# VectorE takes the low halves 4 to 7 in one row with the second norm's statistics behind them, and GpSimd adds the last layer's residual one step later

## What is computed

```python
h = maximum(_layernorm(x), 0);  x = x + elu(softmax(masked leaky_relu(f1 + f2)) @ h)       # first block
h = maximum(_layernorm(x), 0);  y = h
for l in range(3):                                                                       # second block
    attn = softmax(where(mask, leaky(si + sj + b), -inf))
    z = layernorm(y + attn @ y) * g1 + beta1                                             # first norm
    ff = gelu(z @ W1[l] + b1) @ W2[l] + b2
    y = layernorm(z + ff) * g2 + beta2                                                   # second norm
return x + y                                                                             # the residual
```

## Time and profile before

| | us |
|---|---|
| median of three runs | 2756.68 |
| lowest and highest | 2756.49, 2758.12 |
| the profiled execution | 2756.02 |
| its span in the profile | 2754.2 |
| granted TensorE clock, mean | 0.987 |

### The profile page before, as it was taken

How to read it: one execution, slowest core, us unless ns; L and a number is a source line. 1 busy time by engine, 2 the same in 40 slices (tenths; PEclk the granted TensorE clock), 3 DMA queues, 4 the chain that set the end, 5 groups by cost and what they waited for, 6 DMA issues and landing times.

```text
span 2754.2 us, 53331 instructions
## 1 busy us (share of the span) xinstructions
PE 2652.4 (96%) x16771; PEld 2388.7 (87%) x16868; DVE 2139.7 (78%) x7999; ACT 2201.9 (80%) x4494; POOL 1677.8 (61%) x2181
## 2 busy tenths in 40 slices
PE   4699999999999999999999999999999999999997
PEld 3688988898889898988898989898888898998997
DVE  6998787877787877787877888877888767677674
ACT  4889888888888888888887888888888777777774
POOL 4466666557676556566666566555676554454555
PEclk7899999999999999999999999999999999999999
DMA  6222222222122212122322121212132211111121
GB/s 203 75 73 85 70 94 73 77 74 94 63 93 66 77 64 74 51 76 81 100 74 88 45 81 66 78 56 89 60 104 81 68 36 52 42 46 53 50 64 54
DMA packets 118590, 203.43 MB, mean 74 GB/s; under 512 B 12801, under 2 KB 85537, under 8 KB 118305
## 3 DMA queue, kind: packets, MB, share of 16 engines
q1 hardware_dynamic: 118304, 199.97, 22.5%
HBM read 116.05 MB, written 83.89 MB: 73 GB/s over the span
## 4 chain that ended last, share of the span: by engine, by line
PE 72%; DVE 12%; POOL 8%; issue 5%; ACT 2%; DMA 1%; SPq 0%; DVEq 0%; POOLq 0%; ACTq 0%
PE bank L605 33%; PE bank L588 27%; PE ps_u L564 7%; POOL xo L374 3%; DVE g_lo L988 3%; DVE st L962 2%; POOL rs L1295 2%; PE ps_u L646 2%; PE ps_s L559 2%; DVE ub L1081 2%; PE ps_s L551 1%; POOL hb L374 1%; DVE ub L957 1%; ACT g_hi L862 1%; ACT bank L864 1%
## 5 line engine op out<-in xcount | busy, mean ns | idle before, releaser
L605 PE MATMUL bank<-w_hi,g_hi 128*128 128x256 f32 x3072 | 890.9, 290 | 15.4 <-DVE g_lo L988 15.2
L605 PE MATMUL bank<-w_hi,g_lo 128*128 128x256 f32 x3072 | 865.8, 282 | 0.0
L605 PE MATMUL bank<-w_lo,g_hi 128*128 128x256 f32 x3072 | 864.4, 281 | 0.0
L862 ACT ACTIVATE g_hi<-bank,b_eff 128x512 fp32r<-128x512 f32 x768 | 529.7, 690 | 334.2 <-PE bank L588 327.9
L988 DVE TENSOR_TENSOR g_lo<-bank,g_hi 128x512 fp32r<-128x512 f32 x768 | 519.5, 687 | 201.5 <-ACT bank L864 186.2
L588 PE MATMUL bank<-zt_hi,w_hi 128*128 128x512 f32 x1536 | 632.6, 412 | 9.3 <-DVE g_lo L988 5.6
L588 PE MATMUL bank<-zt_hi,w_lo 128*128 128x512 f32 x1536 | 607.4, 395 | 0.0
L588 PE MATMUL bank<-zt_lo,w_hi 128*128 128x512 f32 x1536 | 606.3, 395 | 0.0
L605 PEld LDWEIGHTS bank<-w_hi,g_hi 128*128 128x128 f32 x3072 | 579.5, 189 | 24.1 <-DVE g_lo L988 22.9
L605 PEld LDWEIGHTS bank<-w_lo,g_hi 128*128 128x128 f32 x3072 | 579.8, 189 | 0.8
L605 PEld LDWEIGHTS bank<-w_hi,g_lo 128*128 128x128 f32 x3072 | 579.2, 189 | 0.0
(11 more groups left out here) (96 smaller groups left out, 4141.1 us busy)
## 6 DMA issues: line engine op xcount, KB each, us to landing
xb<-x_scratch SPq DMA_DIRECT2D x88, 512.0 KB, 4.0
x_scratch<-xo SPq DMA_DIRECT2D x64, 512.0 KB, 4.8
xin<-in_x SPq DMA_DIRECT2D x38, 512.0 KB, 4.7
r_scratch<-elu_r SPq DMA_DIRECT2D x32, 512.0 KB, 3.0
xin<-r_scratch SPq DMA_DIRECT2D x32, 512.0 KB, 4.7
out<-xo SPq DMA_DIRECT2D x32, 512.0 KB, 3.6
m<-m_scratch SPq DMA_DIRECT2D x96, 128.0 KB, 3.7
x_scratch<-h SPq DMA_DIRECT2D x24, 512.0 KB, 2.9
```

What stands on the lines that cost most here:

```text
L605: mm = pe.matmul(y, g[:, c, r * P:(r + 1) * P], w[:, l, c, :], start=(c == 0 and n == 0), stop=(c == C - 1 and n == 2))
L862: act.activation(g_hi[:, c, :], block_in, ACT.Gelu, bias=bias).then_inc(g_hi_ready, 1)
```

## The change

In the ordinary step VectorE takes g_low(4) to g_low(7) one behind the other, then the second norm's statistics, a small copy between two scratch tiles, then second_variance and input_variance. GpSimd no longer adds the residual of unit s-1 at the end of step s; it adds that of unit s-2 in step s, behind first_root (and made_root where that comes early) and ahead of scaled_rows. SyncE's program is unchanged.

```diff
                 input_statistics()
                 g_low(4)
                 g_low(5)
+                g_low(6)
+                g_low(7)
                 second_statistics()
-                g_low(6)
+                dve.tensor_copy(spare[:, 2:2 + T], neg_half[:, :])
                 second_variance()
-                g_low(7)
                 input_variance()
                 if v1 is not None and early_step(v1) >= 0:
                     mask_sums(v1)
@@
                 first_root()
                 if v3 is not None and v3 < CH:
                     made_root()
+                if live(s - 2) and s - 2 < U - 1:
+                    residual(pool, st, s - 2)
                 scaled_rows()
@@
                     affine(pool, st, s - 1)
-                    residual(pool, st, s - 1)
```

## The result

The changed kernel takes **2782.16 us** (median of 4 runs, 2780.70 to 2782.73), the kernel before 2756.59 (4 runs). The ratio is 1.0092, 95% interval 1.0079 to 1.0106: slower by 25.6 us, outside the range given. The profiled execution took 2781.81 with a span of 2780.0, so 25.8 of span are to be found; its mean granted clock is 0.985, 0.987 before.

What follows compares the result with a forecast made beforehand. TensorE's own stream, busy 96% of the span, was taken as the bound, so other engines could only return or add waits. Terms 1.5 + 2.9 + 0.65 - 7.5 + 2.25 = -0.2 gave 2756.5 us, range 2741 to 2769.

Steps and rivals of the forecast that it cites:

- The early step's wait: TensorE's wait for g_low(7) in early steps of plain pairs: 0.71 us, to go, leaving early steps at 26.3.
- waits for `vb`: Sign at hidden(1) in middle steps: TensorE's waits grow from 3 cases to some 20, sum near 20 us.
- The plain pairs: 11 early-and-middle step pairs: 0.71 us returned, a new wait of 0.85 paid, +0.14 each, +1.5 in all.
- the tail: Step 95, chain to the last unit: second variance ends later by 2.25 us, hidden by nothing.
- Stalls trade places: Rival 1, early and middle pairs: early wait goes, a `vb` wait replaces it; 2756.5 us, from 2750 to 2763; chance 0.60.
- one element at a time, so I give it no contention: first_norm on VectorE beside the moved residual on GpSimd: 407 ns for 256 elements, no slowdown counted.
- late steps: Steps that keep one length, left out of the loss; VectorE's later work there hidden at the step's end: nothing.
- VectorE has spare time: Steps 75 to 94, which have no first block: the change costs nothing there.
- Rival 3: Residual blocks first_norm in the last layer: g_low(3) 2.1 us late, 1.0 to 1.8 in each of 24 steps, 2790; chance 0.12.
- Together -7.5: Eight last-layer residual pairs: first_root no longer waits, losses of 15.3 us become 6.8, plus 1.0 contention at the copy.
- The late pieces: Pairs 5/6, 8/9, 11/12 with a late weight piece: 0.71 us not got back, whole 0.98 paid, +2.9.
- Pair 47/48: Pair at the loop's branch: the same 0.98 us, less about 0.33 that the residual takes, +0.65.

Runs made afterwards that it cites:

- the row alone: VectorE's new order with the copy, put into the kernel before, the residual left at its old place: 2771.14 us, ratio 1.0055.
- the residual alone: The residual moved behind the first root in the kernel before, VectorE's order as before: 2766.44 us, ratio 1.0034.
- the residual behind first_norm: Changed kernel with GpSimd waiting for `z_ready` ahead of the residual: 2770.16 us in one run (kernel before 2755.91 beside it).
- the fills: Changed kernel with the residual's four additions replaced by one small product and four zero fills of the same rows: 2758.45 us in one run.
- The halves: One half of the change each in the kernel before, VectorE's new order or the residual's new place: 2771.14 and 2766.44 us.

## Why the prediction was wrong

**Right.** The early step's wait goes (26.26). VectorE falls behind by nearly 1 us and `vb` takes the wait over: the row of step 36 above, 23 waits for `vb` where some 20 were forecast, 14.8 us in total for near 20. The plain pairs (+0.8 for +1.5) and the tail (+2.4 for +2.25) came out nearly as worked. "Stalls trade places" describes the 22 steps of the plain pairs, and of the others what is left once the hold of first_norm is taken off.

**The step that failed** is "one element at a time, so I give it no contention". first_norm beside the residual takes 2.64 for 1.37. Three rows settle it: the row alone leaves it at 406 ns, the residual alone brings it to 505, and the residual behind first_norm gives 406 again. The pace of an operation by itself did not tell what it holds or waits for. The nearest row, L957 at 0.95, had the same warning in it, and 2.1 us late for four was worked from it; it was given a chance of 0.12. The Trainium skill ("SBUF — State Buffer", Who interferes with whom) says that a `tensor_scalar` in a two-port mode and a GpSimd operation exclude each other for a whole instruction. The trace agrees as to the hold, also beside GpSimd operations that only write; the double pace of such a mode no run here shows.

Its price, the changed kernel against the residual behind first_norm: 3.9 in late steps, 4.6 in steps 74 to 94, 4.4 in the residual pairs' early steps, and some 9 in their middle steps (the estimate above). That is some 22 of the 25.8, without the pair at the branch. Two terms that the forecast had at nothing, "late steps" left out and "VectorE has spare time" from 75 on, fail by this. Spare time over a step is not room at one place: first_norm, g_low(3) and hidden(7) follow at once. Rival 3 named the mechanism, and its time, 2790, is nearer to the 2782 measured than the forecast is. It was too dear (+33 for some +22): first_norm was not 2.1 but 1.27 late, and some 0.4 to 1.1 of it reached TensorE.

**"Together -7.5"** for the residual pairs came out +5.0. The hold has 4.4 of that in the early steps and some 9 in the middle ones; without it the pairs would be at about -8.4. With a shorter hold, by the fills, they reach -5.9. So the term was about right in itself, and is the second casualty of the first mistake.

**The late pieces**, +2.9 forecast, +5.4 found: the 0.98 paid in full was right, and what was missed is that TensorE, having stood for 1.84 and 2.33 us, went on at granted 0.50 for a stretch. Step 6 had the same 1.84 and step 9 of the row-alone run too, both without a fall (29.32 and 29.34), so it does not follow each time. No term of the forecast had the clock in it.

**Pair 47/48**, +0.65 forecast, +2.9 found: in step 48 the two new waits stand together (2.05 for `vb`, 0.87 for g_low(3)). The halves give +0.4 and +1.9; the 0.6 that they leave was not followed up, nor were the 0.5 us at the start.

Without the hold and the falls, some 22 and 3 us, the span would have been about +1 (an estimate), close to the -0.2 of the sum. So the rest of the sum stood, and the one term put at nothing made the error.

## What to carry to other kernels

Before taking a wait away, follow the in-order work of the engine that is late over the step boundary: if it has no idle time, the wait comes back at its next deadline, and only shortening its chain (work ahead of a wait for another engine) gives time. Before moving an engine's work into a "free" slot, read what runs beside that slot on an engine that it may hold (here VectorE beside GpSimd), and how soon TensorE needs that result. And when two halves of a change add up, look at what ends each wait before giving each half its share: the same wait can have another cause in the whole. The better move here was the same four operations in time in which GpSimd was idle.

## What the hardware showed that was not expected

- An fp32 TENSOR_SCALAR with two per-row scalars, 128 x 256 in SBUF, runs at 407 ns alone and at 660 ns beside GpSimd's two-operand additions; GpSimd's own pace, four in 2.99, was hardly touched (four in 2.8 before). Beside GpSimd's fills, 1.07 us for four, its four take 1.81 to 1.93 instead of 1.37.
- After one wait of 1.84 us in a kernel that keeps TensorE 96% busy, the granted clock fell to 0.50 (1.2 GHz) for a stretch of 3 us in one run and not in another, at about 1.5 us for the step; in a third run it fell after the wait in step 6 and not after that in step 9.
